# Tiles two and four behind: from a product with a level table to two broadcast rows overlaid by a predicated copy

## The reference

```python
def _layernorm(x, axis=-1, eps=1e-05):
    m = jnp.mean(x, axis=axis, keepdims=True)
    v = jnp.var(x, axis=axis, keepdims=True)
    return (x - m) / jnp.sqrt(v + eps)

# attention, with _layernorm(x) as its input; b = 8, t = 1024, D = 128, H = 8 heads of 128, LV = 12 levels
q = (x @ Wq.T).reshape(b, t, H, S)
k = (x @ Wk.T).reshape(b, t, H, S)
v = (x @ Wv.T).reshape(b, t, H, HD)
g = -jax.nn.softplus(x @ Wg.T + bg)
dl = (x @ Wdl.T).reshape(b, t, H, LV)
lam = jax.nn.softplus(dl + Lparam[None, None])
G = jnp.cumsum(g, axis=1)
# level 0: s == t; level l >= 1: t - s in [2^(l-1), 2^l)
lvl, mask = _level_structure(t, LV)
scores = jnp.einsum('bthd,bshd->bhts', q, k) * scale
decay = exp(G[t] - G[s]) where s <= t, else 0
lamw = jnp.einsum('bthl,tsl->bhts', lam, one_hot(lvl))
A = scores * decay * lamw
y = jnp.einsum('bhts,bshd->bthd', A, v).reshape(b, t, H * HD)
out = y @ Wo.T + x            # then a layer norm with ln_g, ln_b

# experts, with _layernorm(x) as their input; 8 experts of 128 x 128
gate = softmax(x @ Wg + bg); the two largest, scaled to sum 1
out = sum over experts of gate * (x @ We[e].T + be[e])

x = x + attention(_layernorm(x))
x = x + experts(_layernorm(x))
```

## Time and profile before

| | |
|---|---|
| median of three runs | 1411.46 us |
| the profiled execution | 1405.15 us |
| its span | 1403.3 us |
| TensorE busy | 1299.5 us, 93% |
| ScalarE busy | 1104.5 us, 79% |
| VectorE busy | 1082.8 us, 77% |
| GpSimd busy | 792.7 us, 56% |
| mean granted TensorE clock | 0.987 of full speed |

### The profile page before, as it was taken

The page is one execution under the profiler, slowest core; times in us unless marked ns, Lnnn a source line. Parts: engine busy times, 40 slices in busy tenths (PEclk is TensorE's granted clock), DMA queues, the critical chain, the costliest instruction groups (busy, mean ns, idle before and its releaser), DMA issues.

```text
span 1403.3 us, 31442 instructions
## 1 busy us (share of the span) xinstructions
PE 1299.5 (93%) x10278; PEld 1137.4 (81%) x10278; DVE 1082.8 (77%) x2724; ACT 1104.5 (79%) x3270; POOL 792.7 (56%) x956
## 2 busy tenths in 40 slices
PE   4699899999999999999999999999999999989997
PEld 4588788888888788787888888887888878878875
DVE  4767767798868977689777988679886797767776
ACT  3589879888788877897788977888778887778732
POOL 2154457734585455953578444864558545595562
PEclk9899999999999999999999999999999999999998
DMA  5311122112221121111221122211212112211200
GB/s 180 113 45 51 43 70 70 42 43 59 58 72 44 50 73 54 44 50 44 73 73 50 44 58 58 67 44 37 71 46 73 50 44 59 72 45 30 67 9 16
DMA packets 125725, 80.37 MB, mean 57 GB/s; under 512 B 50569, under 2 KB 115323, under 8 KB 125435
## 3 DMA queue, kind: packets, MB, share of 16 engines
q1 hardware_dynamic: 124472, 77.85, 20.2%
q10 hardware_dynamic: 1090, 0.51, 0.2%
HBM read 67.64 MB, written 10.09 MB: 55 GB/s over the span
## 4 chain that ended last, share of the span: by engine, by line
PE 47%; ACT 16%; DVE 12%; POOL 11%; SPq 6%; issue 4%; DMA 3%; ACTq 0%; POOLq 0%; DVEq 0%
PE o_ps L1603 11%; ACT w_all L844 6%; PE s_ps L1523 4%; PE l_ps L1546 4%; PE aux L1523 4%; PE s_ps L1525 4%; PE s_ps L1524 4%; POOL a_lo_all L692 4%; PE aux L1524 3%; PE aux L1525 3%; SPq L456 3%; ACT a_hi L892 3%; DVE a_all L1150 2%; PE aux L1616 2%; SPq L469 2%
## 5 line engine op out<-in xcount | busy, mean ns | idle before, releaser
L692 POOL TENSOR_TENSOR a_lo_all<-a_all,a_hi 128x256 fp32r<-128x256 f32 (+2 forms) x576 | 575.5, 1016 | 526.2 <-ACT a_hi L892 524.4
L844 ACT ACTIVATE w_all<-l_ps,bias 128x128 f32<-128x128 f32 x1589 | 439.3, 388 | 43.8 <-PE l_ps L1546 42.4
L1150 DVE TENSOR_TENSOR a_all<-s_ps,w_all 128x512 f32<-128x512 f32 (+3 forms) x768 | 360.6, 483 | 132.6 <-PE s_ps L1525 87.9
L1603 PE MATMUL o_ps<-a_hi,v_all 128*128 128x256 f32 (+2 forms) x1152 | 396.7, 353 | 1.7 <-POOL a_lo_all L692 1.7
L892 ACT ACTIVATE a_hi<-a_all 128x256 fp32r<-128x256 f32 (+2 forms) x576 | 300.1, 547 | 75.5 <-DVE a_all L1150 73.7
L1523 PE MATMUL s_ps<-q_hi,xt_hi 128*128 128x256 f32 (+2 forms) x576 | 224.8, 390 | 31.1 <-DVE a_all L1150 29.3
L1603 PEld LDWEIGHTS o_ps<-a_hi,v_all 128*128 128x128 f32 x1152 | 218.1, 189 | 23.1 <-POOL a_lo_all L692 1.8
L1525 PE MATMUL s_ps<-q_hi,xt_lo 128*128 128x256 f32 (+2 forms) x576 | 195.1, 339 | 0.0
L1524 PE MATMUL s_ps<-q_lo,xt_hi 128*128 128x256 f32 (+2 forms) x576 | 194.7, 338 | 0.0
L1603 PE MATMUL o_ps<-a_lo_all,v_all 128*128 128x256 f32 (+2 forms) x576 | 194.4, 338 | 0.0
L1523 PEld LDWEIGHTS s_ps<-q_hi,xt_hi 128*128 128x128 f32 x576 | 109.8, 191 | 43.9 <-DVE a_all L1150 22.8
(11 more groups left out here) (259 smaller groups left out, 2617.5 us busy)
## 6 DMA issues: line engine op xcount, KB each, us to landing
far<-ef_scratch SPq DMA_DIRECT2D x64, 320.0 KB, 3.6
rb<-eb_scratch SPq DMA_DIRECT2D x1016, 0.8 KB
farther<-ef_scratch SPq DMA_DIRECT2D x64, 192.0 KB, 3.3
ra<-ea_scratch SPq DMA_DIRECT2D x508, 4.0 KB, 2.1
rc<-ea_scratch SPq DMA_DIRECT2D x508, 4.0 KB, 1.6
mt<-m_scratch SPq DMA_DIRECT2D x62, 128.0 KB, 3.5
nt<-n_scratch SPq DMA_DIRECT2D x62, 128.0 KB, 3.5
tx<-in_L_attn_x SPq DMA_DIRECT2D x9, 512.0 KB, 5.6
```

Source lines behind the costliest of these rows:

```text
L692: pool.tensor_tensor(a_lo[r][:, 0:t1 - t0], a[r][:, 0:t1 - t0], a_hi[r][:, 0:t1 - t0].bitcast(F32), ALU.subtract).then_inc(a_lo_done, 1)
L844: last = act.activation(w[k][:, W_AT[j] + d, :].rearrange("p (f c) -> p f c", f=2), l_tiles[:, :, :, i - i0], ACT.Exp, bias=bias[b % 2][:, ...
L1150: dve.tensor_tensor(a[(n * NG + g) % NA][:, 0:t1 - t0], s_ps[:, g % 2, 0:t1 - t0], w[n % 2][:, at:at + (t1 - t0) // P, :].rearrange("p i n ...
L1603: last = pe.matmul(o, lhs[:, vr, j, :], rhs[r][:, 0:t1 - t0], start=fresh, stop=True, skip_group_check=True)
```

## The change

Units 2 and 3 go, with the table `mb2`/`mb4`, the rows `rb`, their DRAM copy and the parts of `level_high` and `low_logs` that made them. In their place three float32 rows of the head are loaded to all partitions: `row8` and `row9` (levels 8 and 9, query tiles 2 to 7) and `row10` (query tiles 4 to 7). Tile 3 is taken from `row9` as it was from `far`. In tile 2 behind (distances 129 to 383), level 8 holds up to 255 and level 9 beyond: a predicated copy on VectorE writes `row9` over `row8` where a constant mask `after` is set. In tile 4 (385 to 639), another writes `row9` over `row10` where `until` is set. Then ScalarE takes the exponentials from these rows: five of `row9`, six of `row8`, four of `row10`, as `row_exps` parts 0, 1 and 2. The three rows have one buffer each; loading head n + 2 waits for all three parts of head n + 1. The place tables are all new.

```diff
-FAR = ((3, 9), (ND, 10))
-FAR0 = FAR[0][0]
 NS = NC - ND
 NQ = NS * P
-NF = (NC - FAR0) * P
+NEAR, TOP = 2, 4
+NR = (NC - NEAR) * P
+NT4 = (NC - TOP) * P
...
-UNITS = [[(0, 0, 8)], [(1, 1, 7)], [(2, 2, 6)], [(4, 4, 4)]]
+UNITS = [[(0, 0, 8)], [(1, 1, 7)]]
...
-    rb = np.arange(KB)
-    l_b, q_b = (rb // 2 % HIGH + LOW)[:, None, None], (rb // (2 * HIGH))[:, None, None]
-    t_b = np.arange(NTB)[None, :, None] * TB + q_b
-    for d in (2, 4):
-        put(f"mb{d}", level(d * P + t_b - s) == l_b)
...
-U_AT = {0: 0, 3: 1, 5: 2, 8: 3}
-FAR_AT = {8: 0}
-B_AT = {21: 0}
-S_AT = {30: 0}
-C_OUT = {31: 0}
-X_AT = {41: 0}
-Q_AT = {8: 0, 21: 1}
-V_AT = {6: 0, 20: 1, 36: 2, 45: 3}
-Q_OUT = {12: 0, 24: 1}
-V_HIGH = {5: 0, 24: 1, 31: 2, 44: 3}
-V_LOW = {14: 0, 29: 1, 41: 2, 52: 3}
...
+U_AT = {0: 0, 4: 1}
+FAR_AT = {3: 0, 6: 1, 9: 2}
+SEL_AT = {15: 1, 20: 0}
+NFAR = 3
+B_AT = {12: 0}
+S_AT = {29: 0}
+C_OUT = {32: 0}
+X_AT = {42: 0}
+Q_AT = {8: 0, 23: 1}
+V_AT = {8: 0, 26: 1, 36: 2, 45: 3}
+Q_OUT = {11: 0, 23: 1}
+V_HIGH = {7: 0, 23: 1, 28: 2, 46: 3}
+V_LOW = {13: 0, 30: 1, 40: 2, 52: 3}
...
-            213: [('log', 0)], 218: [('log', 1)], 228: [('up', 2)], 232: [('l_low', 0)], 236: [('decay', 0)],
-            240: [('up', 3)], 242: [('l_low', 1)], 244: [('up', 4)], 259: [('up', 5)], 274: [('up', 6)],
...
+            172: [('gate', 2)], 178: [('softplus', 0), ('softplus', 1)], 190: [('guard', 0)], 192: [('gate', 3)],
+            195: [('up', 0)], 198: [('sums', 0)], 214: [('up', 1)], 222: [('log', 0)], 227: [('up', 2)],
...
-        rb = [sb(f"rb{k}", [KB, TB, NTB, NC], F16) for k in range(2)]
-
-        far = [sb(f"far{k}", [P, NF]) for k in range(2)]
-        farther = [sb(f"farther{k}", [P, NF - (FAR[1][0] - FAR0) * P]) for k in range(2)]
+        row8, row9, row10 = sb("row8", [P, NR]), sb("row9", [P, NR]), sb("row10", [P, NT4])
+        after, until = (sb(n, [P, P], U8) for n in ("after", "until"))
+        farther = [sb(f"farther{k}", [P, NQ]) for k in range(2)]
...
-        def load_rb(eng, n, qs):
-            b, h = divmod(n, H)
-            for q in qs:
-                eng.dma_start(rb[n % 2][q * 2 * HIGH:(q + 1) * 2 * HIGH, q, :, :],
-                              eb_dram[b, h * HIGH:(h + 1) * HIGH, :, q * T // TB:(q + 1) * T // TB]
-                              .rearrange("l r (t i) -> (l r) t i", i=NC)).then_inc(rb_in[n % 2], 16)
-
         def store_el_far(eng, b):
             eng.dma_start(ef_dram[b], el_far).then_inc(t["stored"], 16)
 
-        def load_far(eng, n):
+        def load_rows(eng, n):
             b, h = divmod(n, H)
-            eng.dma_start(far[n % 2][:, :], ef_dram[b, h * HIGH + FAR[0][1] - LOW, :].partition_broadcast(P)).then_inc(
-                far_in[n % 2], 16)
+            for level, row in ((8, row8), (9, row9), (10, row10)):
+                at = NR - row.shape[1]
+                eng.dma_start(row[:, :], ef_dram[b, h * HIGH + level - LOW, at:].partition_broadcast(P)).then_inc(rows_in, 16)
...
-                    load_rb(sp, n, range(TB))
-                    if n >= 2:
-                        sp.wait_ge(far_done, n - 1)
-                    load_far(sp, n)
+
+                def load_next_rows(n):
+                    sp.wait_ge(far_done, NFAR * n)
+                    sp.wait_ge(t["stored"], EL * (n // H + 1))
+                    load_rows(sp, n)
...
+                        load_next_rows(n + 2)
                         load_next_farther(n + 2)
...
-                def far_exps(n):
+                def row_exps(n, part):
                     k = n % 2
                     b, h = divmod(n, H)
-                    act.wait_ge(far_in[k], 16 * (n // 2 + 1))
-                    for j in range(NC - FAR0):
-                        last = act.activation(w[k][:, W_AT[j] + FAR0, :], far[k][:, j * P:(j + 1) * P], ACT.Exp,
-                                              bias=bias[b % 2][:, h, BIAS_AT[FAR0] + j:BIAS_AT[FAR0] + j + 1])
+                    d, row = ((3, row9), (NEAR, row8), (TOP, row10))[part]
+                    if part == 0:
+                        act.wait_ge(rows_in, ROWS_IN * (n + 1))
+                    else:
+                        act.wait_ge(selected[part - 1], n + 1)
+                    first = NC - row.shape[1] // P
+                    for j in range(NC - d):
+                        at = (j + d - first) * P
+                        last = act.activation(w[k][:, W_AT[j] + d, :], row[:, at:at + P], ACT.Exp,
+                                              bias=bias[b % 2][:, h, BIAS_AT[d] + j:BIAS_AT[d] + j + 1])
...
-                    for r0, r1, q in EL_ROWS:
-                        act.activation(permuted(elt_hi, r0, r1, q, f),
-                                       bank(piece)[r0:r1, :].rearrange("r (i t q) -> r q t i", q=q, i=HC),
-                                       ACT.Copy).then_inc(t["el_hi"], 1)
+                    act.activation(permuted(elt_hi, 0, NA_ROWS, TA, f),
+                                   bank(piece)[0:NA_ROWS, :].rearrange("r (i t q) -> r q t i", q=TA, i=HC),
...
-                far_exps(0)
+                for part in range(NFAR):
+                    row_exps(0, part)
...
-                            far_exps(n + 1)
+                            row_exps(n + 1, FAR_AT[g])
...
-                        dve.wait_ge(far_done, n + 1)
+                        dve.wait_ge(far_done, NFAR * (n + 1))
...
+                def select_rows(n, part):
+                    dst, src, where = ((row8, row9, after), (row10, row9, until))[part]
+                    dve.wait_ge(rows_in, ROWS_IN * (n + 1))
+                    tiles = dst.shape[1] // P
+                    dve.copy_predicated(dst[:, :].rearrange("p (i n) -> p i n", n=P),
+                                        where[:, None, :].broadcast_to([P, tiles, P]),
+                                        src[:, NR - tiles * P:].rearrange("p (i n) -> p i n", n=P)).then_inc(selected[part], 1)
...
-                    for part, (r0, r1, q) in enumerate(EL_ROWS):
-                        dve.wait_ge(t["el_hi"], b * 4 + f * 2 + part + 1)
-                        dve.tensor_tensor(permuted(elt_lo, r0, r1, q, f),
-                                          bank(piece)[r0:r1, :].rearrange("r (i t q) -> r q t i", q=q, i=HC),
-                                          permuted(elt_hi, r0, r1, q, f),
-                                          ALU.subtract).then_inc(freed(piece) if part else t["el_lo"], 1)
+                    dve.wait_ge(t["el_hi"], b * 2 + f + 1)
+                    dve.tensor_tensor(permuted(elt_lo, 0, NA_ROWS, TA, f),
+                                      bank(piece)[0:NA_ROWS, :].rearrange("r (i t q) -> r q t i", q=TA, i=HC),
+                                      permuted(elt_hi, 0, NA_ROWS, TA, f), ALU.subtract).then_inc(freed(piece), 1)
...
+                dve.wait_ge(preds, 2)
+                for part in range(2):
+                    select_rows(0, part)
...
+                        if place in SEL_AT and n + 1 < NH:
+                            select_rows(n + 1, SEL_AT[place])
...
-                    if u == 2:
-                        pe.wait_ge(rb_in[k], RB_IN * (n // 2 + 1))
...
-                        if d <= 1:
-                            for tb in range(NTA):
-                                f, at = divmod(tb * TA, HF)
-                                last = mm(f, l_bank[f][:, at:at + TA, :], m(f"ma{d}")[:, tb * P:(tb + 1) * P],
-                                          (ra, rc)[d][k][:, :, tb, i0:i0 + cnt])
-                        if d in (2, 4):
-                            for tb in range(NTB):
-                                f, at = divmod(tb * TB, HF)
-                                last = mm(f, l_bank[f][:, at:at + TB, :], m(f"mb{d}", KB)[:, tb * P:(tb + 1) * P],
-                                          rb[k][:, :, tb, i0:i0 + cnt])
+                        for tb in range(NTA):
+                            f, at = divmod(tb * TA, HF)
...
-                    if u < 2:
-                        value(0, u + 2)
-                    if u in (2, 3):
-                        scores(0, u - 2)
-                    if u == 3:
-                        for k in range(Q_U):
-                            query(1, k)
+                    value(0, u + 2)
+                for g in range(2):
+                    scores(0, g)
+                for k in range(Q_U):
```

92 lines of the change are left out of this document (42 added, 50 removed), and 13 rows, old and new, of tables (DVE_MORE, PE_MORE).

## The result

The changed kernel took **1431.5 us** in the median of four runs (1430.4 to 1434.1), beside 1411.0 of the kernel before on the same chip: ratio **1.0147**, interval 1.012 to 1.0173. It is 20.5 us slower; 4.6 us faster was forecast. The profiled execution has a span of 1428.6 us.

A forecast was written before the change was run, and what follows sets the result against it. No engine alone bounds it: five of eight heads follow TensorE, two VectorE, one GpSimd. -30 - 8 + 19.7 + 5.3 + 8.4 = -4.6 us, so 1406.9 us; own range 1396 to 1420, 8 in 10 1378 to 1436.

The forecast's parts named there:

- products and burst: TensorE loses 0.75 us in 40 heads, -30 us; fewer exponentials in the burst before the next head's first weighing, -8.
- moved side work: In h3 and h4, side work moved in and out was said to cancel: 0 us.
- late rows: At the start of h5, rows queued behind SyncE's level stores land late: 1.2 us in seven elements, +8.4 us.
- copies, VectorE's time: In h3 and h4, where VectorE sets the pace, 1.64 us a pair in six elements: +19.7 us (bounds 9.8 and 39.4).
- Waiting for GpSimd: Copies in h1, h3 and h4 held by GpSimd subtractions, half counted for GpSimd's pause: +5.3 us (bounds nothing and 10.6).
- What VectorE takes on: Two predicated copies a head, 1.64 us a pair, unhidden in h3 and h4 (+19.7 us), hidden behind TensorE in other heads.
- rival three: Predicated copies also stop GpSimd, in h0 and h1: 19.7 us more and full waiting of 10.6, 1432 us; chance 0.17.
- TensorE's gain and the exponentials: Products of tiles 2 and 4 gone from TensorE, -30 us over 40 heads; shorter burst of exponentials on ScalarE, -8.
- the second term: Shorter ScalarE burst before the next head's first weighing, 1.3 us in one VectorE wait an element, six times: -8 us.

The follow-up runs named there:

- rows_first_no_copies: Changed kernel without its two predicated copies (overlay left out) and with the row loads issued ahead of the level stores: 1379.0 us, ratio 0.9771.
- rows_first: Changed kernel with SyncE issuing the loads of the rows and of `farther` ahead of the next element's level stores, both copies kept: 1419.8 us, ratio 1.0073.
- no_copies: Changed kernel without its two predicated copies (overlay left out); ScalarE's row exponentials wait for the rows' landing instead: 1389.8 us, ratio 0.986.
- memset_same_time: Changed kernel with each predicated copy replaced by a VectorE fill of a spare tile, 1.52 us a head, reading no SBUF: 1408.7 us, ratio 0.9978.
- old_side_rows_first_no_copies: Changed kernel without predicated copies, side work at its old places, rows loaded ahead of the level stores: 1375.8 us, ratio 0.9757.
- until_later: Changed kernel with rows loaded ahead of the level stores, `after` copy kept at place 20, `until` copy moved from 15 to 30: 1450.5 us, ratio 1.0285.

## Why the prediction was wrong

| step | forecast | measured | from |
|---|---|---|---|
| products and burst | -38 | -35 | 1375.8, beside 1410.9 |
| moved side work | 0 | +3 | 1379.0 less 1375.8 (with copies -1) |
| late rows | +8.4 | +11 | 1389.8 less 1379.0 (with copies +12) |
| copies, VectorE's time | +19.7 | +19 | 1408.7 less 1389.8 |
| copies, VectorE and GpSimd waiting for each other | +5.3 | +23 | 1431.5 less 1408.7 |
| sum | -4.6 | +21 | |

**The steps that failed** are two. By size it is the term "Waiting for GpSimd", below: +5.3 forecast, 23 measured, 17.5 of the 25 us between forecast and result. By place it is this, in "What VectorE takes on": "In the other heads VectorE has 3.6 us of air or more and the pair lies behind TensorE." The length of a copy was right (1.56 us a pair by pitch, 1.64 forecast; the line of the earlier trace rows gives 0.97 for the longer one where 0.95 was written). That the time came to 19 us for 19.7 is luck, since it does not fall where it was charged. Head by head over the six middle elements, us from `rows_first_no_copies` to `rows_first`, beside what was forecast for time and lock:

| | h0 | h1 | h2 | h3 | h4 | h5 | h6 | h7 | first and last element |
|---|---|---|---|---|---|---|---|---|---|
| forecast | 0 | +2.7 | 0 | +11.1 | +11.1 | 0 | 0 | 0 | 0 |
| measured | +8.2 | +14.1 | +4.2 | -4.0 | +0.7 | +2.8 | +2.0 | +4.1 | +11.1 |

h3's -4.0 is nearly all clock: the kernel without copies has the drop in all six elements there, the one with them in three, at 1.2 us each. Of h1's +14.1 some 6 are clock: elements without a drop differ by 1.3 us (22.2 and 20.9). So in h3 and h4, where VectorE is busiest, the copies cost nothing; in `no_copies` VectorE waits for TensorE 0.87 and 0.49 us in h4 just where they stand. They cost where VectorE had 3.6 us of air and more, and so do the fills, which lock nothing: from `no_copies` to `memset_same_time` h0 grows by 4.1, h1 by 6.5 (most of it clock) and h7 by 2.2 us over the six elements, h3 and h4 by 1.6 and 0.7. Busy time over a head says nothing of play within it: VectorE stands between TensorE's scores and ScalarE's, GpSimd's and TensorE's next steps twelve times a head, and its air lies in other places than the copies. By the fills, between 0.90 and 1.52 us a head is where it gives out.

**Waiting for GpSimd** was put at 5.3 us, because the places "lie in GpSimd's pause". GpSimd held the `until` copy in 26 of 64 heads. VectorE's own waits, 13.5 us, exceed even the bound of 10.6. GpSimd's waits for the copies were left to rival three; h1 shows them, and TensorE's stand behind them. Rival three gave 1432 and had the mechanism that cost most, 23 us of locking where it put 30. That its number is so close is luck: it charged VectorE's time to h3 and h4 too, and its other terms were too low by 8.

**The moved side work.** "The moved side work cancels there" was wrong for the heads it named and right for the sum. `up` 3 entered h4 too, which I had not counted, and `l_low` 1, which I had, begins 0.1 us before h4 ends. What I had at nothing is the same locking: three steps of the moved `log` work take 3.6 us in h4 of every middle element where the kernel before has them at 0.8. One of them, in the changed kernel and then in the kernel before (ns min/median/max):

```profile
L1237 DVE TENSOR_TENSOR z<-lz,run_far x8: 160/1250/1253, 31.0 to 1165.5; 128x24 f32<-128x24 f32 x8
L1242 DVE TENSOR_TENSOR z<-lz,run_far x8: 154/162/166, 31.0 to 1136.2; 128x24 f32<-128x24 f32 x8
```

They read two SBUF tiles, and at their new places GpSimd is at its subtractions (478.04 to 479.36 and 482.67 to 486.25 in the element shown). They do the same in `no_copies`. h4 pays 5.5 us in each of six elements, 33 in all, and VectorE's sum over h3 and h4 rose from 40.3 to 45.3 us; what left h1, h2, h5 and h6 pays it back. Read alone, the changed trace says that h4 is the whole loss; the experiments say it is none of it.

**Late rows**: mechanism and place were right (once an element, at h5, behind the level stores, landings about 6 us after issue), the size was 11 or 12 instead of 8.4. `farther`, queued behind the rows, was as late as they: of ScalarE's 30.3 us of waiting for it 21.5 go with `rows_first`.

**TensorE's gain and the exponentials** came near in sum, -35 for -38, and in part by luck. At the old places without the burdens the six middle elements are 2.7 us each shorter (h5 alone 1.4), 16.4 in all where the two terms had 30; the first and last elements together give 13.6 us where they had 7.5. And the second term is hardly in it. In this kernel, `old_side_rows_first_no_copies`, the exponentials are spread as in the changed one, but VectorE waits for them almost as long as in the earlier trace rows:

```profile
DVE a_all L1136 <- ACT w_all L842: 25.3, 12, 4.9
```

At the start of h3 the wait is 2.24 us in each element, 2.35 before. There a ScalarE step of 0.9 us, `abs` (128x832), stands ahead of the last four exponentials; the new places put it behind them, and the wait is gone (1.3 us in the changed kernel). As far as these three kernels show, it takes both, the spreading and the new place. What the wait's end is worth in time was not measured by itself.

## What to carry to other kernels

Before an engine's air is counted as cover, look for it between the two instructions where the new one will stand: a busy share over a head hid 0.9 us a head here and not 1.5. An instruction with two SBUF inputs on VectorE costs in its own time, in what it holds of GpSimd, and, if it comes second, in what is left of GpSimd's instruction, at worst of its whole unbroken run; put it where GpSimd is known to pause. A stand-in for an instruction is as long as the starts of the rows around it say, not its own row. A stretch that grew between two traces is not the cause until its price is taken away alone: h4 grew by 33 us, and the places that made it grow are worth 3 at most.

## What the runs showed of the hardware

- A predicated copy of float32 under a broadcast uint8 mask takes 742 ns for 512 columns and 1042 for 768: 1.17 ns a column and 0.14 us at the start.
- The row of a fill shows 0.83 ns a column (608 ns for 660, 848 for 948), but VectorE is idle before it by 0.2 ns a column more (147 ns for 948, 198 for 1183): 1.04 ns a column in all. In f16 with an even count it was recorded as a uint32 fill of half the length (551 ns for 1182), with an odd count not (1044 ns for 1183). The Trainium skill, page "VectorE: DVE Perf Modes", section "Zero memsets can be issued as uint32 (trn2)", names a whole number of 4-byte words as a condition, and the trace agrees.
- A GpSimd TENSOR_SCALAR with one SBUF tile as input was held by VectorE's predicated copy, to 1230 ns from 447.
- A VectorE copy with two SBUF inputs waited through five GpSimd instructions in a row, 5.15 us for 0.74, in h1 of `until_later`; in h0 of the changed kernel it got in between two of a row, 1.60 us.
- TensorE's clock was seen to fall to 1.2 GHz about 1 us after it took up work from a stand of 3.15 us, and to stay there for 3.2 us. After the same stand, in another element, it kept 2.4 GHz.
